# A two-layer recurrence of 128 steps: another first step, splits and casts spread over later steps, loops that turn elsewhere

## What is computed

```python
# layer 0, an LSTM
a = x_t @ Wx + b + h @ Wh              # 4 gates of 128
i, f, o, g = sigmoid(a_i), sigmoid(a_f), sigmoid(a_o), tanh(a_g)
c = f * c + i * g;  h = o * tanh(c)
x1_t = x_t + h
# layer 1, a UGRNN
m = concat(x1_t, u) @ weight + bias
g = sigmoid(m_g + 1); c = tanh(m_c)
u = g * u + (1 - g) * c
out_t = x1_t + u
```

## Time and profile before

| | |
|---|---|
| runs | 232.51, 232.40, 231.21 us |
| profiled execution | 231.32 us, of which the span from first to last instruction is 229.7 |
| TensorE busy (matmuls) | 223.8 us, 97% |
| weight loads | 207.4 us, 90% |
| VectorE | 201.5 us, 88% |
| ScalarE | 121.5 us, 53% |
| GpSimd | 4.4 us, 2% |
| granted TensorE clock, mean | 0.994 |

### The profile page before, as it was taken

One profiled execution on the slowest core, in us unless ns is written; L12 is line 12 of the kernel. 1 busy time (PEld: TensorE's weight loads), 2 busy tenths in 40 slices (PEclk: granted clock), 3 DMA queues, 4 the chain that ended last, 5 costly groups with the idle time before them and its releaser, 6 DMA issues.

```text
span 229.7 us, 12849 instructions
## 1 busy us (share of the span) xinstructions
PE 223.8 (97%) x4850; PEld 207.4 (90%) x4850; DVE 201.5 (88%) x1557; ACT 121.5 (53%) x778; POOL 4.4 (2%) x12
## 2 busy tenths in 40 slices
PE   7999999999999999999999999999999999999994
PEld 5799999999999998999999999999999999999882
DVE  6788989988889898899888998998989989899894
ACT  3645555555555555555555555555555555555551
POOL 1500000000000000000000000000000000000000
PEclk9999999999999999999999999999999999999997
DMA  6000001010010001000010000100001000000000
GB/s 191 18 16 27 14 27 49 14 30 24 15 45 23 11 23 44 23 14 23 23 35 23 23 11 23 46 11 23 23 18 40 23 22 13 27 14 14 16 16 11
DMA packets 11970, 6.22 MB, mean 27 GB/s; under 512 B 1446, under 2 KB 11692, under 8 KB 11948
## 3 DMA queue, kind: packets, MB, share of 16 engines
q1 hardware_dynamic: 11792, 5.66, 8.7%
q10 hardware_dynamic: 156, 0.27, 0.3%
HBM read 3.82 MB, written 2.10 MB: 26 GB/s over the span
## 4 chain that ended last, share of the span: by engine, by line
PE 72%; DVE 19%; ACT 3%; DMA 1%; issue 1%; SPq 1%
PE a L284 14%; PE gate_f L258 11%; PE a L242 7%; PE a L276 6%; PE gate_o L226 4%; PE gate_i L226 4%; PE gate_g L226 4%; DVE cell_bank L572 3%; PE gate_f L226 3%; PE gate_g L264 3%; PE gate_o L264 3%; PE gate_i L264 3%; ACT act_bank L487 3%; PE gate_i L268 2%; PE a L278 2%; DVE hT L579 2%
## 5 line engine op out<-in xcount | busy, mean ns | idle before, releaser
L258 PE MATMUL gate_f<-hT,wh_raw 128*128 128x32 f32 x254 | 49.0, 275 | 0.2
L258 PEld LDWEIGHTS gate_f<-hT,wh_raw 128*128 128x128 f32 x254 | 37.8, 188 | 11.6 <-DVE hT L579 8.2
L472 ACT ACTIVATE forget<-gate_f 128x32 f32<-128x32 f32 x127 | 25.0, 197 | 36.9 <-PE gate_f L258 36.7
L492 ACT ACTIVATE acts<-a 128x64 f32<-128x64 f32 x128 | 28.6, 223 | 28.1 <-PE a L284 28.1
L579 DVE TENSOR_TENSOR hT<-out_gate,act_bank 128x32 f32<-128x32 f32 x128 | 24.1, 188 | 21.6 <-ACT act_bank L487 21.6
L487 ACT ACTIVATE act_bank<-cell_bank 128x32 f32<-128x32 f32 x128 | 23.3, 182 | 35.5 <-DVE cell_bank L572 35.5
L276 PE MATMUL a<-h_high,w1x_part 128*128 128x32 f16 x768 | 41.8, 176 | 0.3 <-ACT w1x_part L464 0.2
L284 PE MATMUL a<-acts,w1h_part 128*128 128x32 bf16 x762 | 39.3, 178 | 0.0
L572 DVE TENSOR_TENSOR_SCAN cell_bank<-scan_mul,scan_add 128x64 f32<-128x64 f32 x128 | 38.7, 302 | 0.4 <-ACT scan_add L472 0.3
L278 PE MATMUL a<-h_low,w1x_fp 128*128 128x32 f16 x256 | 35.4, 176 | 0.0
L284 PEld LDWEIGHTS a<-u_rest,w1h_part 128*128 128x128 bf16 x508 | 31.4, 98 | 1.5
(11 more groups left out here) (96 smaller groups left out, 631.7 us busy)
## 6 DMA issues: line engine op xcount, KB each, us to landing
xT<-in_x_dram SPq DMA_DIRECT2D x46, 64.0 KB, 1.8
out_dram<-outT SPq DMA_DIRECT2D x32, 64.0 KB, 1.6
wx_s<-in_L_cond_Wx_dram SPq DMA_DIRECT2D x1, 256.0 KB, 2.8
wh_raw<-in_L_cond_Wh_dram ACTq DMA_DIRECT2D x1, 256.0 KB, 3.1
w_raw<-in_L_cond_weight_dram SPq DMA_DIRECT2D x1, 256.0 KB, 3.6
bias_rows<-in_biases_dram ACTq DMA_DIRECT2D x1, 3.0 KB
condT<-in_cond_dram SPq DMA_DIRECT2D x1, 16.0 KB, 2.9
```

The source lines that it names most:

```text
L258: nc.tensor.matmul(gate_step(GATE_F, j), wh_raw[:, GATE_F * P:(GATE_F + 1) * P], hT[:, (j - 1) % RING, :], start=False, stop=True, skip_gr ...
L472: return nc.scalar.activation(out, gate_step(q, j), func)
L492: nc.scalar.activation(acts1[:, 0:3:2, i, :], a1_step(j).rearrange("p (g n) -> p g n", g=2), ACT.Tanh).then_inc(acts1_ready, 1)
```

## The change

- *First step.* i, g and o of step 1 are fp32 products with Wh as it came (`second_state`), and layer 1's step 0 is four fp32 products with its weights as they came (`layer1_step0`), for which POOL halves cond. Layer 1's step 1 takes its state as fp32 from the scaled weights.
- *First projections.* Those of i, g and f cover 3, 4 and 3 steps, gate o's 4, so that all come from x's first piece. The fills of steps 2 to 7 are written out (`fill_first`), and layer 1's projections for steps 8 to 15 move to steps 8 to 11.
- *Splits and casts.* Layer 1's scaling on ACT goes behind the tanh of step 0 and around that of step 1; its four casts to bf16 move to steps 2 to 5. Until then (`early`) TensorE reads the first two bf16 parts as the upper halves of the fp32 words, with a stride of two elements. DVE's last split of Wh and the two casts to fp16 move one step later.
- *Order of the fills.* The banks begin at steps 1, 3, 5 and 7 for f, i, g and o, which were 7, 1, 3 and 5.
- *Turns.* TensorE does the gates of the next body's first step before it turns. DVE turns before the last `layer1_low` of a body. The waits for x and for output slots stand behind the scan of an earlier step, and `add_layer0` and `add_layer1` swap places.
- *Warm-up.* 15 products from a tile of ones that DVE writes, in place of 12 from the identity.

The diff, cut to what these points name:

```diff
-BEGIN = (7, 1, 3, 5)
+BEGIN = (1, 3, 5, 7)
...
-WARM = 12
+WARM = 15
...
+            nc.gpsimd.tensor_scalar(cond_half[:, :], condT[:, :], 0.5, None, ALU.mult).then_inc(half_ready, 1)
...
+            def second_state(q, done):
+                nc.tensor.matmul(gate_step(q, 1), wh_raw[:, q * P:(q + 1) * P], hT[:, 0, :],
+                                 start=False, stop=True, skip_group_check=True).then_inc(done, 1)
...
+            def three(parts, scaled, rest, q, early):
+                columns = slice(q * P, (q + 1) * P)
+                if early:
+                    return upper(scaled[:, columns]), upper(rest[:, columns]), parts[:, 2, columns]
+                return [parts[:, w, columns] for w in range(3)]
...
+            def layer1_step0():
+                for q, weights in enumerate((w1x_gate[:, :], w1_raw[:, 0, P:2 * P])):
+                    nc.tensor.matmul(a1_step(0)[:, q * N:(q + 1) * N], weights, x1T[:, 0, :],
+                                     start=q == 0, stop=False, skip_group_check=True)
+                bias1(0, 0)
+                pe.wait_ge(half_ready, 1)
+                for q, moving in enumerate((cond_half[:, :], condT[:, :])):
+                    mm = nc.tensor.matmul(a1_step(0)[:, q * N:(q + 1) * N], w1_raw[:, 1, q * P:(q + 1) * P], moving,
+                                          start=False, stop=True, skip_group_check=True)
+                mm.then_inc(a1_summed, 1)
+            def layer1_step1_state():
+                pe.wait_ge(u_ready, 2)
                 pe.wait_ge(w1_scaled, 2)
                 for q in range(2):
-                    mm = nc.tensor.matmul(a1_step(0)[:, q * N:(q + 1) * N], w1h_scaled[:, q * P:(q + 1) * P],
-                                          u_of(RING - 1), start=False, stop=True, skip_group_check=True)
+                    mm = nc.tensor.matmul(a1_step(1)[:, q * N:(q + 1) * N], w1h_scaled[:, q * P:(q + 1) * P],
+                                          u_of(0), start=False, stop=True, skip_group_check=True)
                 mm.then_inc(a1_summed, 1)
...
-            project0(GATE_I, 0, 1)
-            bias0(GATE_I, 0, 1)
-            project0(GATE_G, 0, 3)
-            bias0(GATE_G, 0, 3)
+            project0(GATE_I, 0, 3)
+            bias0(GATE_I, 0, 3)
+            project0(GATE_G, 0, 4)
+            bias0(GATE_G, 0, 5)
             pe.wait_ge(wh_in, 16)
             pe.wait_ge(cond_in, 16)
             first_state(GATE_I, i_summed)
             first_state(GATE_G, g_summed)
-            pe.wait_ge(x_in[1], 16)
-            project0(GATE_O, 0, 5)
-            bias0(GATE_O, 0, 5)
+            project0(GATE_O, 0, 4)
+            bias0(GATE_O, 0, 7)
             first_state(GATE_O, o_summed)
-            project0(GATE_F, 1, 6)
-            bias0(GATE_F, 1, 6)
-            pe.wait_ge(w1_gate_ready, 1)
-            project1(0, 0, 0, 0)
+            project0(GATE_F, 1, 3)
+            bias0(GATE_F, 1)
+            def fill_first(j, s):
+                if j == 2:
+                    pe.wait_ge(x_in[1], 16)
+                    pe.wait_ge(scan_in_ready, 2 * s + 1)
+                    project0(GATE_I, 3, HS)
+                    bias0(GATE_I, 3)
+                if j == 3:
+                    pe.wait_ge(scan_in_ready, 2 * s + 1)
+                    project0(GATE_G, 4, 1, False)
+                    pe.wait_ge(o_ready, s + 1)
+                    project0(GATE_O, 4, 3, False)
+                    pe.wait_ge(x_in[2], 16)
+                    pe.wait_ge(f_ready, s)
+                    project0(GATE_F, 4, 5, False)
+                if j == 4:
+                    pe.wait_ge(scan_in_ready, 2 * s + 1)
+                    project0(GATE_G, 5, HS)
+                    bias0(GATE_G, 5)
+                if j == 6:
+                    pe.wait_ge(scan_in_ready, 2 * s + 1)
+                    project0(GATE_I, 7, HS, False)
+                    pe.wait_ge(o_ready, s + 1)
+                    project0(GATE_O, 7, HS)
+                    bias0(GATE_O, 7)
+                if j == 7:
+                    pe.wait_ge(x_in[3], 16)
+                    pe.wait_ge(scan_in_ready, 2 * s + 1)
+                    project0(GATE_G, 9, HS, False)
+                    pe.wait_ge(o_ready, s + 1)
+                    project0(GATE_O, 11, HS, False)
+            def gates(s, j, first):
+                pe.wait_ge(h_ready, s)
+                forget_sum(j)
+                if first and j == 1:
+                    pe.wait_ge(high_ready, s)
+                    second_state(GATE_I, i_summed)
+                    second_state(GATE_G, g_summed)
+                    second_state(GATE_O, o_summed)
+                    return
+                if first and j == 2:
+                    pe.wait_ge(wh_split, 4)
+                pe.wait_ge(high_ready, s)
+                high(GATE_I, j)
+                if first and j == 2:
+                    pe.wait_ge(fp16_ready, 1)
+                pe.wait_ge(low_ready, s)
+                low(GATE_I, j, i_summed)
+                high(GATE_G, j)
+                low(GATE_G, j, g_summed)
+                high(GATE_O, j)
+                low(GATE_O, j, o_summed)
             def body(s0, first, last):
...
+                    if j > 0:
+                        gates(s, j, first)
+                    early = first and j < 6
+                    if first and j == 1:
+                        pe.wait_ge(x1_ready, 1)
+                        pe.wait_ge(w1_gate_ready, 1)
+                        layer1_step0()
+                    if first and j == 6:
+                        pe.wait_ge(w1_cast, 4)
+                    if first and j == GS + 1:
+                        project1(1, 1, 0, GS)
+                        bias1(1, 0)
+                    if not (first and j < 2):
+                        pe.wait_ge(acts1_ready, s - 1)
+                        if first and j == 2:
+                            project1(0, 0, 1, 1, 3)
+                            project1(1, 0, 1, 1, 3)
+                        if first and j == 5:
+                            project1(0, 0, HS, HS)
+                            project1(1, 0, HS, HS)
+                            bias1(0, 1)
+                        if first and j == GS + 2:
+                            project1(0, 1, HS, GS + HS)
+                        if first and j == GS + 3:
+                            project1(1, 1, HS, GS + HS)
+                            bias1(1, 1)
+                        if first and j == 2:
+                            pe.wait_ge(w1_scaled, 1)
                             pe.wait_ge(w1_split, 2)
                             pe.wait_ge(fp16_ready, 2)
...
+                    if fills and k == 0:
                         if m == 0:
                             pe.wait_ge(x_in[0], s0 + 16)
                             pe.wait_ge(x_in[1], s0 + 16)
+                        pe.wait_ge(f_ready, s)
+                        project0(GATE_F, a, a_steps)
+                    if fills and k == 1:
+                        if not ends:
+                            pe.wait_ge(x_in[2 if m == 0 else 4], s0 + 16)
+                        pe.wait_ge(f_ready, s)
+                        project0(GATE_F, b, b_steps, False)
...
+                    if first and j == GS:
+                        project1(0, 1, 0, GS, begins=True)
+                if not last:
+                    gates(s0 + BODY, 0, False)
...
-                    if first and j < 2:
-                        split_layer1(2 * j)
+                    if first and j == 1:
+                        scale_layer1(1)
                     state(s)
-                    if first and j < 2:
-                        split_layer1(2 * j + 1)
+                    if first and j == 0:
+                        scale_layer1(0)
+                    if first and j == 1:
+                        scale_layer1(2)
+                    if first and 2 <= j < 6:
+                        cast_layer1(j - 2)
...
+            nc.vector.memset(idle[:, :], 1.0).then_inc(idle_ready, 1)
...
             def body(s0, first):
+                if not first:
+                    layer1_low(s0 - 3, BODY - 3)
                 for j in range(BODY):
                     s = s0 + j
                     l0, l1, l2 = [(j - back) % BODY for back in (1, 2, 3)]
                     layer1_runs = not (first and j < 2)
                     if not (first and j == 0):
                         hidden(s - 1, l0)
-                        add_layer0(s - 1, l0, s0 + 16 if j else s0)
+                    if not (first and j < 3):
+                        add_layer1(l2)
+                    if not (first and j == 0):
                         hidden_low(s - 1, l0)
                     if first and j == 1:
+                        add_layer0(0, 0)
+                        last_part()
+                    if first and j == 2:
                         dve.wait_ge(w1_scaled, 1)
                         to_fp16(w1x_fp16[:, :], w1x_scaled[:, :])
                     if layer1_runs:
```

(16 more changed lines are left out.)

166 lines of the change are left out of this document (67 added, 99 removed).

## The result

The kernel after took 236.83 us (median of 4 executions, 234.85 to 237.97) against 232.38 before (231.21 to 232.51): ratio 1.020, 95% interval 1.016 to 1.024. The forecast was 232.2, its range ended at 234.1. Executions over 1.5% longer than the fastest of the same kernel are left out of ratios and of what is called undisturbed (four of nine in e1, at 240.63 to 241.35, four of eight in e9, five of ten in e12); where one was profiled (e2, e9, e11, e13), TensorE's products stay at half pace for 17 to 24 us from the start.

What follows compares the result with a forecast made beforehand. The recurrence, 1.69 us a step, was taken to bound the kernel, with TensorE never far from full. Start -0.15, entry -0.07 and -0.01 made -0.2, so 232.2 against the median 232.4; 8-in-10 range 229.9 to 234.1.

Steps and rivals of the forecast that it cites:

- The start: First hidden states: hT of step 0 at 6.8 instead of 7.53, of step 1 at 9.1 instead of 9.90.
- three extra warm-up products: TensorE's warm-up at the start: 0.57 us of products, costed at nothing, 0.36 at worst.
- TensorE's sums: Product times added per step after step 1: hT of step 4 0.9 earlier, shrinking to about 0.15 by later crowding.
- POOL's subtractions: Step 1: they hold up VectorE operations with two SBUF inputs; 0.4 added together with a cast, nothing to 0.6.
- The crowding of steps 8 to 11: Layer 1's moved projections beside regular fills: steps of 1.67, 1.97, 1.78 and 1.97 against 1.69; 0.63 to about 0.75 lost.
- my sums for steps 5 to 7: TensorE's work in those steps, 1.67, 1.67 and 1.56, taken as covered by the recurrence, so no loss.
- The turns: Loop's backward turns: 0.22 each against 0.21 before, nothing won there, 0.07 won at the loop's entry.
- The rival's 0.36 more per turn: Loop turns: late u_low and late input cost 5 x 0.36 = 1.8, giving 233.9 to 234.7; chance 0.15.
- the first rival: Start and turns: both gains stay, turns hidden by queued work, -2.0 to 230.4, up to -2.5; chance 0.23.
- Strided weights: Weight loads in steps 2 to 5: taken as free; the rival at fp32 price, up to 4.2, 235 to 236, chance 0.04.

Runs made afterwards that it cites:

- e1: The changed kernel with twelve idle 256-column warm-up products where TensorE waited in steps 0 to 2; undisturbed 233.33 to 233.98 us, ratio to before 1.007.
- e9: e8 with gate o's first projection cut to four steps, from x's first piece, the fifth following in step 0; ratio 0.9945.
- e12: The kernel before, with TensorE's work between first state and step 1 made thin, same products in all; undisturbed ratio 1.001.
- e2: e1 with TensorE and VectorE turning where they did before the change; undisturbed median 233.0 us, ratio 1.0045.
- e11: e1 with POOL's four subtractions replaced by memsets to zero; no time given, profile at half pace until about 24 us.
- e13: The kernel of e11 run once more for a full-pace profile, again at half pace until about 24 us; undisturbed median 233.24 us.
- e15: e13 without the third group of idle products, between gate i's high and low product of step 2; undisturbed median 232.9 us, ratio 1.003.
- e6: e1 with fills of steps 3 to 11 spread, the old turning places, and the waits of e3; undisturbed median 231.78 us, ratio 0.999.
- e5: e1 with gate o's fills of steps 6 and 7 moved behind layer 1's last product of the same step; undisturbed median 233.35 us.
- e3: e1 with VectorE's waits on x and output buffers back at the residual sums, in written-out bodies only; undisturbed median 233.0 us, ratio 1.0047.
- e8: The kernel before with VectorE's waits on x and output buffers moved behind the scan, in the loop only; median 231.29 us, ratio 0.998.

## Why the prediction was wrong

- **The start** was right: hT of step 0 at 6.91 (6.8 forecast), of step 1 at 9.29 (9.1). x's second piece is not waited for. That it came so close is partly luck: the same start gave 6.38 to 7.49 in other runs. The three extra warm-up products, which I took as free, have TensorE's first projection begin at 4.35 instead of 4.05, within the 0.36 that I allowed at worst.
- **The step that failed is "TensorE's sums".** Its prices were those of the earlier trace rows, and they hold at full clock only. In step 5 of after the two projections and the bias, by start time, are:

```profile
18.26 0.77 PE L247 MATMUL a<-xT,w1x_gate 128*128 128x128 f32 x2
18.83 0.64 PE L247 MATMUL a<-xT,w_raw 128*128 128x128 f32 x2
19.25 0.42 PE L252 MATMUL a<-pick,bias_lhs 128*128 128x256 bf16 x1
19.47 0.23 PE L293 MATMUL a<-h_high,w1x_scaled 128*128 128x32 f16 x1
```

  0.99 for the pair and 0.22 for the bias, where I had 0.60 and 0.11. I costed what the change moves out of steps 0 to 2 by what it adds later, and nothing for what it leaves behind: a TensorE too thin to keep its clock. hT of step 4 came at 17.02 instead of 14.75; 1.1 of that is the half clock (10.11 for e1's 9.00), and with the 1.5 of steps 5 to 12 it makes 2.6 of the 5.1.
- **The same step, at full clock.** Steps 1 to 4 took 9.00 in e1 for my 7.95: I gave POOL's subtractions 0.4 in step 1, with a cast, and none in step 2, where e15 is 0.46 and 0.70 shorter (0.94 over the four steps). Step 4 took 2.22 where I had about 1.65; e6, with gate f's piece of step 3 moved behind, has 1.92, and the rest is open. Steps 5 to 12 lost 1.5 where I had 0.75 lost. The crowding of steps 8 to 11 came as I summed it: 1.67, 1.97, 1.78 and 1.97, and the steps to hT 9 to 12 took 1.68, 2.07, 1.80 and 1.96 in e1, 0.76 lost. The other 0.76 came where I had nothing: my sums for steps 5 to 7 were 1.67, 1.67 and 1.56, "which the recurrence covers"; the steps to hT 6, 7 and 8 took 1.97, 1.91 and 1.95. I had left out layer 1's loop, in which it matters where in a step a product stands; e5 shows that for 0.42 of the 0.76.
- **The turns** were nearly right: 0.24 to 0.3 a turn for my 0.22, from u_low 0.35 late (0.15 to 0.35 forecast). The rival's 0.36 more per turn did not come. The Trainium skill (Advanced Engine Details and Errata, Sequencer and Instruction Queues) says that engine instructions can be queued while a control instruction runs; that this hides a turn, as the first rival had it, is not borne out by the 0.25 of issue in front of u_low.
- **The written-out bodies** I left out: 0.07 for each even step, 8 times in the last body, 0.5 (e3).
- **Strided weights** cost at most 5 ns a load: in e1, by line and tile, x count, busy us, mean ns:

```profile
L293 PEld LDWEIGHTS a<-h_high,w1x_part 128*128 128x128 bf16 x746 | 31.2, 96 | 0.7 <-ACT acts L592 0.4
L293 PEld LDWEIGHTS a<-h_high,w1x_scaled 128*128 128x128 bf16 x8 | 0.8, 101 | 0.0
L293 PEld LDWEIGHTS a<-h_high,w1x_rest 128*128 128x128 bf16 x8 | 0.8, 97 | 0.0
```

  The first is packed, the other two have the stride: that rival is out, and what the Trainium skill says (TensorE: Matmul & The Clock Gate, Weight-path perf modes) agrees.
- None of the rivals named the clock. One that did would have needed two readings that were open to me: TensorE's busy share of each microsecond of the start, and what of it the change takes away.

## What to carry to other kernels

Work taken off TensorE is not only a saving, since its granted clock can fall: where a start is thinned out, look at what keeps TensorE busy there, and fill or leave it. A sum of busy times bounds a step from below only; where two recurrences share the engines, walk both, and note on which side of each loop's last product a fill stands. The same wait behaved in opposite ways here: at the residual sums it cost 0.07 us once after each turn of the loop (e8) and nothing in the written-out bodies (e3), behind the scan nothing in the loop and 0.07 in every even step of the written-out bodies. Why is not shown, but a loop and its written-out copies have to be looked at apart.

## What was not expected of the hardware

Idle products made a kernel faster: twelve of them in steps 0 to 2 took 3 us off (e1, 233.46 for 236.41 in the profiled executions).

The granted clock is not the whole of TensorE's pace at the start. e13's page has it at full speed throughout,

```profile
PEclk9999999999999999999999999999999999999999
```

but at 12.29 four idle products of 256 columns take 1.04 together, 0.21 apart, where e1's (6.41) take 0.60, 0.11 apart:

```profile
12.29 1.04 PE L339 MATMUL a<-idle 128*128 128x256 bf16 x4
```

So pace is read from products of a known size, not from that column alone. What decides how long the first half pace lasts is open.
